# Packed edge ranges and two late transposes in the edge-counting stage of a graph network

## The reference

```
msgs  = feat[src]
neigh = segment_sum(msgs, dst, 1250)
rst   = (1 + eps) * feat + neigh
h     = relu(rst @ W1 + b1) @ W2 + b2 + feat
```

## Time and profile before

| | us |
|---|---|
| median of 3 runs | 1729.66 (1729.47 to 1729.70) |
| the profiled execution's own time | 1729.81 |
| its span, first to last instruction | 1728.1 |
| TensorE busy | 1708.2 (99%) |
| VectorE busy | 1214.8 (70%) |
| ScalarE busy | 802.9 (46%) |
| GpSimd busy | 555.1 (32%) |

### The profile page before, as it was taken

One profiled execution on the slowest core, in us unless ns is written; L12 is line 12 of the kernel. 1 busy time (PEld: TensorE's weight loads), 2 busy tenths in 40 slices (PEclk: granted clock), 3 DMA queues, 4 the chain that ended last, 5 costly groups with the idle time before them and its releaser, 6 DMA issues.

```text
span 1728.1 us, 32350 instructions
## 1 busy us (share of the span) xinstructions
PE 1708.2 (99%) x11894; PEld 1511.2 (87%) x11894; DVE 1214.8 (70%) x2229; ACT 802.9 (46%) x1325; POOL 555.1 (32%) x880
## 2 busy tenths in 40 slices
PE   8999999999999999999999999999999999999998
PEld 7998788889999888889998888899988888999887
DVE  7996559457786875477878673677776835778676
ACT  5668332136665331256663412466644123666531
POOL 1002613312334732023337340133363401333473
PEclk9999999999999999999999999999999999999999
DMA  4003311311111303121113122111131312112222
GB/s 136 1 1 150 116 49 44 127 71 40 47 59 38 96 32 129 40 67 45 47 32 105 48 89 80 47 46 62 32 100 36 109 41 79 34 46 62 70 92 73
DMA packets 64779, 113.08 MB, mean 65 GB/s; under 512 B 15318, under 2 KB 25686, under 8 KB 64640
## 3 DMA queue, kind: packets, MB, share of 16 engines
q1 hardware_dynamic: 64640, 111.22, 19.7%
HBM read 89.19 MB, written 22.00 MB: 64 GB/s over the span
## 4 chain that ended last, share of the span: by engine, by line
PE 98%; DVE 1%; issue 0%; DVEq 0%; DMA 0%; SPq 0%; ACT 0%; POOLq 0%; POOL 0%; ACTq 0%
PE ps L1565 61%; PE ps L1625 16%; PE ps L1720 7%; PE ps L1512 6%; PE ps L1542 3%; PE ps L1652 2%; PE ps L1666 2%; DVE masked_s L1272 1%; PE ps L1482 0%; DVEq L426 0%; PE ps L1581 0%; DMA idx_rows<-in_dst_dram 0%; PE ps L1576 0%; PE ps L1463 0%; DVE hot L1097 0%
## 5 line engine op out<-in xcount | busy, mean ns | idle before, releaser
L1256 DVE TENSOR_TENSOR pT<-ps,pT 128x640 fp32r<-128x640 f32 (+1 forms) x320 | 243.9, 804 | 153.9 <-ACT pT L1016 153.8
L1565 PE MATMUL ps<-yT,w 128*128 128x512 f32 (+1 forms) x1728 | 330.0, 352 | 0.0
L1016 ACT CAST pT<-ps 128x640 fp32r<-128x640 f32 (+1 forms) x320 | 202.4, 685 | 252.9 <-PE ps L1720 247.1
L1565 PEld LDWEIGHTS ps<-yT,w 128*128 128x128 f32 x1728 | 280.6, 189 | 44.8
L1565 PE MATMUL ps<-kh,q_parts 128*128 128x512 f32 (+3 forms) x1440 | 310.5, 360 | 5.4 <-DVE small L1272 5.4
L1565 PEld LDWEIGHTS ps<-kh,q_parts 128*128 128x128 f32 (+1 forms) x1440 | 243.0, 186 | 51.1 <-issue 3.7
L1565 PE MATMUL ps<-w,kh 128*128 128x512 f32 (+1 forms) x960 | 235.4, 396 | 0.0
L1625 PE MATMUL ps<-pT,v 128*128 128x256 f32 (+3 forms) x1600 | 215.6, 281 | 0.0
L953 ACT ACTIVATE s<-masked_s,small 128x1250 f32 (+1 forms) x156 | 211.2, 1354 | 0.0
L1565 PEld LDWEIGHTS ps<-w,kh 128*128 128x128 f32 (+1 forms) x960 | 173.7, 186 | 38.9 <-DVE q L1283 1.8
L1625 PEld LDWEIGHTS ps<-pT,v 128*128 128x128 f32 (+1 forms) x1600 | 200.3, 190 | 0.0
(11 more groups left out here) (189 smaller groups left out, 2534.4 us busy)
## 6 DMA issues: line engine op xcount, KB each, us to landing
mask<-mask_dram SPq DMA_DIRECT2D x24, 640.0 KB, 5.1
x_spill<-x SPq DMA_DIRECT2D x36, 256.0 KB
x<-x_spill SPq DMA_DIRECT2D x36, 256.0 KB, 4.3
rep<-rec_dram SPq DMA_DIRECT2D x64, 128.0 KB, 3.3
w_raw<-in_L_gnn_m_w_dram SPq DMA_DIRECT2D x8, 1024.0 KB, 6.4
mask_y<-mask_dram SPq DMA_DIRECT2D x12, 640.0 KB, 5.3
mask_dram<-mask_out SPq DMA_DIRECT2D x10, 640.0 KB, 2.9
w_l<-in_L_gnn_W_dram SPq DMA_DIRECT2D x2, 2048.0 KB, 13.5
```

Of the source, the lines that this page charges most:

```text
L1016: nc.scalar.copy(pT[:, 0, turned_places(gh, half), k * P:k * P + R], turn_bank(half, R)).then_inc(p_high, 1)
L1256: nc.vector.tensor_tensor(pT[:, 1, places, k * P:k * P + R], turn_bank(half, R), pT[:, 0, places, k * P:k * P + R].bitcast(F32), ALU.subtr ...
L1565: mine = mm(to, left(a), right(b), start=first and n == 0, stop=final and n == 2)
```

## The change

The edge ranges are packed otherwise. `table` becomes ten int16 (first edge tile and quads alone), so that one 32-bit word holds two node tiles; an engine reads one word first and four later. `before` is no longer in the table: the product with `earlier` is gone, and each engine adds up the quads itself (`groups_before`). The largest number of quads goes through `four_groups` to the third word of `group_table`, and TensorE reads one word before the first quad and two behind it. TensorE turns three tiles of x ahead of the `bounds` products, five behind them, and the last two behind the first quad; ScalarE copies these two at the end of block 0. ScalarE touches its table early, through a copy of one element, and copies the turned `src` and `dst` as each arrives.

```diff
-        table = sb("table", [1, NT + 1], I32)
-        group_table = sb("group_table", [1, 4], I32)
+        table = sb("table", [1, NT], mybir.dt.int16)
+        group_table = sb("group_table", [1, 3], I32)
...
+        def load_edge_tiles(engine, first_pair, pairs):
+            _, packed = nc.values_load_multi_w_load_instructions(table[0:1, 2 * first_pair:2 * (first_pair + pairs)].bitcast(I32),
+                                                                 engines=(engine,), min_val=0, max_val=2 ** 30 - 1)
+            return list(packed)
-        def edge_tiles(eng, packed):
-            first = eng.snap(packed & (QUADS_AT - 1)).with_bounds(min_val=0, max_val=NE - 1)
-            quads = eng.snap((packed >> 8) & (BEFORE_AT // QUADS_AT - 1)).with_bounds(min_val=1, max_val=NE // HOT + 1)
-            before = eng.snap(packed >> 14).with_bounds(min_val=0, max_val=NT * (NE // HOT + 1))
-            return first, quads, before
+        def edge_tiles(eng, packed, j):
+            at = packed[j // 2] >> 16 if j % 2 else packed[j // 2]
+            first = eng.snap(at & (QUADS_AT - 1)).with_bounds(min_val=0, max_val=NE - 1)
+            quads = eng.snap((at >> 8) & 63).with_bounds(min_val=1, max_val=NE // HOT + 1)
+            return first, quads
+
+        def groups_before(eng, before, quads):
+            return eng.snap(before + quads).with_bounds(min_val=0, max_val=NT * (NE // HOT + 1))
...
-            act.wait_ge(consts, 4)
-            act.wait_ge(idx_t, 2)
+            act.wait_ge(consts, 6)
+            nc.scalar.copy(dst_gap[0:1, 0, 0:1], ident[0:1, 0:1])
             for a in range(2):
+                act.wait_ge(idx_t, 1 + 2 * a)
                 nc.scalar.copy(edge[:, a, 0:NE], ps[0:ET, a, 0:NE]).then_inc(edges_ready, 1)
...
                 if j == 0:
-                    for t in range(6, NT):
+                    for t in range(6, NT - 2):
                         turned_x(t)
...
                 with act.Fori(1, quads) as k:
                     dst_hots(j, act.snap(first + k * HOT), act.snap(before + k))
+                if j == 0:
+                    for t in range(NT - 2, NT):
+                        turned_x(t)
                 nc.scalar.copy(x_high[0:rows(j), j, :], x[0:rows(j), j, :]).then_inc(x_high_done, 1)
...
-            chain(nc.vector.scalar_tensor_tensor(parts[:, 0, :], parts[:, 1, :], float(QUADS_AT), parts[:, 0, :], ALU.mult, ALU.add))
-            nc.vector.scalar_tensor_tensor(table[:, 0:NT], parts[:, 2, :], float(BEFORE_AT), parts[:, 0, :], ALU.mult, ALU.add).then_inc(tiles_s, 1)
-            chain(nc.vector.tensor_reduce(most[:], parts[:, 1, :], AX.X, ALU.max))
-            nc.vector.tensor_copy(group_table[:, 3:4], most[:]).then_inc(most_ready, 1)
+            nc.vector.scalar_tensor_tensor(table[:], parts[:, 1, :], float(QUADS_AT), parts[:, 0, :],
+                                           ALU.mult, ALU.add).then_inc(tiles_s, 1)
+            dve.wait_ge(groups_clear, 1)
+            nc.vector.tensor_reduce(four_groups[:, NT:NT + 1], parts[:, 1, :], AX.X, ALU.max).then_inc(most_ready, 1)
...
-            packed = load_edge_tiles(mybir.EngineType.DVE, FIRST_LOAD)
+            packed = load_edge_tiles(mybir.EngineType.DVE, 0, 1)
+            before = 0
             for j in range(NT):
-                first, quads, before = edge_tiles(dve, packed[j])
+                first, quads = edge_tiles(dve, packed, j)
                 if j == 0:
-                    hots(j, first, dve.snap(before * HOT))
-                    packed += load_edge_tiles(mybir.EngineType.DVE, LATER_LOADS)
+                    hots(j, first, 0)
+                    packed += load_edge_tiles(mybir.EngineType.DVE, 1, PAIRS - 1)
                 with dve.Fori(1 if j == 0 else 0, quads) as k:
                     hots(j, dve.snap(first + k * HOT), dve.snap((before + k) * HOT))
+                before = groups_before(dve, before, quads)
...
-            for t in range(4):
+            for t in range(3):
...
-            for t in range(4, NT):
+            for t in range(3, NT - 2):
...
+            load_groups(0, 1)
+
+            def behind_first_groups():
+                turn_x(NT - 2)
+                turn_x(NT - 1)
+                load_groups(1, 2)
```

More of the change, by code:

```diff
@@ L338, in gnn_kernel @@
         tl_i32 = at("yp", 21504, "tl_i32", [NT, NE], I32)
-        parts = at("yp", 24896, "parts", [1, 3, NT])
-        most = at("yp", 25024, "most", [1, 1])
+        parts = at("yp", 24896, "parts", [1, 2, NT])
         four_groups = at("yp", 25056, "four_groups", [1, 12])
@@ L410, in gnn_kernel @@
         EXACT = 4096
-        CONSTS = 12
-        QUADS_AT, BEFORE_AT = 2 ** 8, 2 ** 14
+        CONSTS = 10
+        QUADS_AT, PAIR_AT = 2 ** 8, 2 ** 16
         TILES_DONE = 9
@@ L417, in x_piece @@
             return x_in_s[n], 32 if n == NG - 1 else 16
[L419 to L429, removed]
-        def edge_tiles(eng, packed):
-            first = eng.snap(packed & (QUADS_AT - 1)).with_bounds(min_val=0, max_val=NE - 1)
-            quads = eng.snap((packed >> 8) & (BEFORE_AT // QUADS_AT - 1)).with_bounds(min_val=1, max_val=NE // HOT + 1)
-            before = eng.snap(packed >> 14).with_bounds(min_val=0, max_val=NT * (NE // HOT + 1))
-            return first, quads, before
+        PAIRS = NT // 2
+        def load_edge_tiles(engine, first_pair, pairs):
[9 more added lines that the diff above has]
+            return eng.snap(before + quads).with_bounds(min_val=0, max_val=NT * (NE // HOT + 1))
         @block.sync
@@ L668, in _ @@
             pool.wait_ge(parts_ready, 1)
+            pool.wait_ge(most_ready, 1)
             pool.sem_inc(passed)
@@ L851, in counts_copy @@
                                ).then_inc(counts_out, 1)
-            packed = load_edge_tiles(mybir.EngineType.Activation, FIRST_LOAD)
+            packed = load_edge_tiles(mybir.EngineType.Activation, 0, 1)
+            before = 0
             for j in range(NT):
-                first, quads, before = edge_tiles(act, packed[j])
+                first, quads = edge_tiles(act, packed, j)
                 dst_hots(j, first, before)
                 if j == 0:
-                    for t in range(6, NT):
+                    for t in range(6, NT - 2):
                         turned_x(t)
-                    packed += load_edge_tiles(mybir.EngineType.Activation, LATER_LOADS)
+                    packed += load_edge_tiles(mybir.EngineType.Activation, 1, PAIRS - 1)
                 if j:
@@ L864, in _ @@
                     dst_hots(j, act.snap(first + k * HOT), act.snap(before + k))
+                if j == 0:
+                    for t in range(NT - 2, NT):
+                        turned_x(t)
                 nc.scalar.copy(x_high[0:rows(j), j, :], x[0:rows(j), j, :]).then_inc(x_high_done, 1)
-            counts_copy(NT - 1, act.snap(before + quads))
+                before = groups_before(act, before, quads)
+            counts_copy(NT - 1, before)
             def rst_high_part(m, g):
@@ L1489, in _ @@
             pe.wait_ge(bounds_ready, 1)
-            for a, (value, onto) in enumerate(((0, ident), (1, ident), (1, earlier))):
-                mine = mm(ps[0:1, 5, a * NT:(a + 1) * NT], bounds[:, value:value + 1], onto[0:NT, 0:NT], start=True, stop=True)
+            for a in range(2):
+                mine = mm(ps[0:1, 5, a * NT:(a + 1) * NT], bounds[:, a:a + 1], ident[0:NT, 0:NT], start=True, stop=True)
             mine.then_inc(bounds_turned, 1)
-            for t in range(4, NT):
+            for t in range(3, NT - 2):
                 if t == 7:
@@ L1496, in _, with count_block @@
                 turn_x(t)
-            def count_block(j, place, quads, before):
+            def count_block(j, place, quads, before, behind_first=None):
                 pe.wait_ge(counts_out, j + 1)
@@ L1516, in count_block @@
                 quad(before, True)
+                if behind_first:
+                    behind_first()
                 with pe.Fori(1, quads) as k:
@@ L1527, in _ @@
                 quads = pe.snap((fours[j // 4] >> 6 * (j % 4)) & 63).with_bounds(min_val=1, max_val=NE // HOT + 1)
-                count_block(j, j % 2, quads, before)
+                count_block(j, j % 2, quads, before, behind_first_groups if j == 0 else None)
                 before = pe.snap(before + quads).with_bounds(min_val=0, max_val=NT * (NE // HOT + 1))
-            most_quads = fours[3]
+            most_quads = pe.snap((fours[2] >> 12) & 63).with_bounds(min_val=1, max_val=NE // HOT + 1)
             pe.wait_ge(counts_out, NT + 1)
```

20 lines of the change are left out of this document (9 added, 11 removed).

## The result

| | before | after |
|---|---|---|
| median, us | 1729.66 (1729.47 to 1731.34, 5 runs) | **1757.84** (1757.54 to 1758.29, 5 runs) |
| profiled execution, its own time | 1729.81 | 1757.84 |
| its span | 1728.1 | 1755.5 |

The changed kernel is 1.6% slower: ratio 1.0163, 95% interval 1.0152 to 1.0174. The forecast was 1758.

What follows compares the result with a forecast made beforehand. TensorE was taken to bound the kernel, with VectorE's sequencer becoming the limit in the counting loops: 1729.8 - 2.85 (opening) + 0.5 (ScalarE's copies) + 31 (loops) = 1758.5, so 1758 us, range 1749 to 1773.

Steps and rivals of the forecast that it cites:

- The reading of the loops: VectorE's counting loops: block j recomputes the running quad number in every quad, j instruction pairs, hidden only up to 2.24 us.
- The loop's term: Counting stage, blocks 1 to 9: added sequencer steps make quads late, 31 us lost, bounds 23 to 44.
- my prices: VectorE's sequencer: 1.83 us for today's quad, plus 0.125 per added ISA and 0.085 per ALU_OP, gaps included.
- the chain's last step: VectorE's running sum: its last step has four results, so 1 us was added to the 30.0 us loop loss.
- an added ISA: VectorE's loops: each added ISA instruction taken as 0.079 us like L1111, 0.125 with its gap.
- The opening: Before the second counting quad: first quad at 13.6, second at 16.8 us against 19.65, 2.85 us gained.
- the two words read behind the first quad lie beside the moved turns: TensorE's opening: its sequencer is ahead, so these reads are hidden; if not, the opening gains 2.0 us.
- ScalarE's copies: End of block 0: two tile copies of 0.49 us each delay ScalarE's one-hots, 0.5 us lost once in block 1, between 0 and 0.8.
- Opening and copies together gain 2.35 us: Kernel without the loop's loss: opening's 2.85 us gain less the copies' 0.5 us, leaving 1727.5 us.
- The chain stays hidden: Rival, VectorE's loops: its sequencer works far enough ahead that added steps are free; 1727.5 us, chance 0.05.
- Once a block: Rival, VectorE's loops: the sum runs only on entering each block, costing 6.3 us in all; 1733.8 us, chance 0.03.
- The clock: Rival, TensorE: rests drop its clock to 1.2 GHz, another 27 us over blocks 5 to 9; 1786 us, chance 0.03.

Runs made afterwards that it cites:

- the held sum: Changed kernel with VectorE's running sum written to its own register ahead of each block's loop, no step inside; 1730.09 us, ratio to before 1.0001.
- the chain alone: Kernel before with one edit: VectorE adds up the running number of quads itself instead of taking it from the packed word; 1749.89 us, ratio 1.0115.
- the run begun anew at block 5: Changed kernel with VectorE's running sum written to a register once, ahead of block 5, so the chain restarts there; 1737.43 us, ratio to before 1.0045.
- the run with the copies in block 3: Changed kernel with the running sum in a register ahead of each loop, ScalarE's two late x copies moved from block 0's end to block 3's; 1729.79 us.

## Why the prediction was right, point by point

**The reading of the loops** held at every step. The running sum is in the loops of blocks 1 to 9, it lies on the sequencer between two quads, and it is free until a quad's steps reach TensorE's time. The run with the held sum shows that it is the loss (27.8 of 28.2 us), the run with the chain alone that nothing else is needed, and the run begun anew at block 5 that there is a threshold.

**The loop's term**: 31 us forecast. From the stage (29.6) comes off 0.65 for ScalarE: 28.9 measured. (Against the held sum the stage is 28.2 longer, 137.2 against 109.0.) Block 2, forecast to lose nearly nothing at 2.25, has 2.35. From block 3 on, forecast against the pitch in the changed kernel: 2.55 and 2.46 (block 3), 2.67 and 2.70, 2.97 and 3.06, 3.09 and 3.04, 3.39 and 3.26, 3.51 and 3.72, and in block 9 3.81 and 3.66. In block 9 the 19 added instructions cost 1.83 us where I had 1.98, 8% too much; blocks 5 and 8, whose excess my prices do not contain, gave some of it back, and the 1 us added for the chain's last step cannot be told apart in the measured pitches. The value that I took for an added ISA, 0.125 with its gap, fits this chain's steps of 82 ns. For the plainer chain in the kernel before it is too high, and there I missed by 5 us. The size of the term is therefore right within a tenth, partly by errors that cancel.

**The opening**: parts copy 10.1 (forecast 10.3), one-hots 11.8 (12.0), first quad 14.03 (13.6), second quad 17.12 (16.8). So 2.5 us in place of 2.85. The term mis-sized is TensorE's group table: I moved GpSimd's six steps forward at their old lengths, and did not ask what VectorE does at that time now. That the two words read behind the first quad lie beside the moved turns came true, with little to spare: TensorE's last register step ends at 17.07 us, and the quad begins at 17.12.

**ScalarE's copies**: 0.5 forecast; in block 1 the pitch is 2.37 where it was 2.24, 0.65 us, and the run with the copies in block 3 shows that they are the cause.

**What I did not have**: 0.5 to 0.6 us outside the span and 0.4 us behind the neighbour sums. In the end 28.65 forecast and 28.0 measured is partly luck: the opening brought 0.3 less, the loops cost 2.1 less, and 1 us came that no step had. It matters for the smaller question. "Opening and copies together gain 2.35 us" was wrong: with the loops mended the change stands at 1730.09, level with before.

**The rivals.** *The chain stays hidden*: no, the stage lost 29.6 us. By the Trainium skill's depth of eight instructions ("Advanced Engine Details and Errata", Engine Queue Depths) the added steps could have hidden behind queued work. They hide only in the room that is left up to 2.24 us (one pair: 2.26 us in block 6 of the chain begun anew); no run shows more of them hidden. A likely reason is that each one-hot waits for a place of `hot` that TensorE frees one at a time, which leaves little to queue up; that was not tried by itself. *Once a block*: no, every quad of a block is late alike (in block 7 the quads come 3.21 us and four times 3.24 behind the ones before them). *The clock*: the products of a quad take 2.47 us behind rests of over 1 us, where half the clock would make it some 4.5, and the profile's granted clock for the execution is 0.999.

## What to carry to other kernels

A value that is computed ahead of a hardware loop but used only inside it may be worked out in the loop, with the whole expression behind it. List the loop's body on the engine and count its register steps; each is some 0.08 to 0.12 us here, and a short loop has room for few. A running value belongs in a register that is written once ahead of the loop. And before work is moved off an engine's path, look whether the engine rests there anyway: turns that filled a hole cost nothing, and with their copies on ScalarE cost some 1 us once moved. Of all versions the packed ranges with the held sum and the tiles left where they were has the lowest median, 1728.92 us, but its interval (0.9985 to 1.0003) does not exclude no difference.

## What the runs showed of the hardware

**VectorE and GpSimd.** A GpSimd step of 0.18 us takes 0.33 to 0.55 when it meets a one-hot of 1280 columns on VectorE. It ends 0.03 to 0.05 us behind it.

**Where a loop lies.** Moved by eight or sixteen instructions, the same loop on VectorE's sequencer takes 2.57 or 2.83 us a round (block 4), and 3.08 or 2.84 (block 5).

**The pace of TensorE's turns** of x goes from 0.21 to 0.11 us each at a moment that differs between executions, from 10.5 to 13.0 us in the profiles of these kernels. The 20 turns behind the bounds took 2.79 us in the changed kernel and 3.75 with the held sum; 28 of them took 3.25 in one kernel and 4.52 in another whose turns are the same. The two paces are a factor of two apart, as the clock's two levels of 1.2 and 2.4 GHz are, but the profile's rows grant 1.00 on either side of the moment, so no row shows the clock to be the cause; it is open. This moves the first quad by up to 0.5 us, and with it what an execution of these kernels takes; differences of under 1 us between openings are not to be read from one profile. In the held sum's profile it accounts for the 0.46 us by which the second quad is late against the changed kernel: the first quad begins 0.16 later, behind the turns, and takes 2.69 us in place of 2.39, because ScalarE's one-hots come late behind its copies of them.

**TensorE at the beginning of a block** loses 0.06 us more in the kernels with the change's TensorE program where VectorE does not set the pace: with the held sum, against before, the starts of the quads slip by that at 40, 52, 63, 85, 97, 108 and 119 us. 0.4 us in all. I did not look for its cause.
